# Phase features without GpSimd, tails added ahead of the query split, and context tiles on lasting semaphores, in a four-layer transformer kernel

## Chip, cores and metric

The kernel runs on one NeuronCore of a Trainium2 chip. The metric is the device time of one execution in microseconds (us). An execution is one launch of the whole network, and a time given as a median is that of three executions.

## What is computed

The reference takes x (32 sequences of 32 tokens, 256 channels, so 1024 tokens) and a context (32 sequences of 257 rows of 192 channels) through four layers. Each layer adds a cross attention, a self attention and a feed-forward part to x, each behind a layer norm. Three places matter here.

```python
# L0_attn: scores with a phase part, per head of 16 channels
q_amp = softplus(q) / sqrt(mean(softplus(q)**2) + 1e-6)        # k_amp likewise
q_phi = pi * tanh(x @ Wqp)                                     # k_phi likewise
phase = (q_amp*cos(q_phi)) @ (k_amp*cos(k_phi)).T + (q_amp*sin(q_phi)) @ (k_amp*sin(k_phi)).T
scores = (q @ k.T + 0.5*tanh(lambda_raw) * phase) / 4

# L2_xattn: softmax attention over the 257 context rows, 8 heads of 64 channels
out = softmax((x @ Wq) @ (context @ Wk).T / 8) @ (context @ Wv) @ Wo + bo

# L3_xattn: the same kind with one head of 256 channels
out = softmax((x @ Wq + bq) @ (context @ Wk + bk).T / 16) @ (context @ Wv + bv)
```

## The kernel before

The program is a row of stages. A stage is a block in which each engine has its own list of instructions with semaphore waits written out by hand. All engines end a stage together and the next one then begins. Tokens lie 128 to a tile (NT = 8 tiles of BT = 4 sequences). The function prepare (from L388) does the layer norm, the turn to channel-major form and the projections ahead of most stages. Its sync engine (SP) runs load_early (L376): it issues the transfers listed in early, then fetches a later stage's weights (fetch_weights, L240), and at L385 waits until all the early transfers have landed. That wait is part of the stage, so no engine goes on before it is over.

**phase_features** (L1630, in L0_attn) works on tensors of 128 partitions by 2048 elements, one for queries (u = 0) and one for keys (u = 1). VectorE (DVE) takes |q| (L1646), ScalarE (ACT) takes tanh of the phases (L1686) and exp of minus |q| (L1689), and DVE makes 1 + exp and its rounding error (L1649, L1652). ACT takes Ln (L1693), DVE adds the parts to the amplitude (L1656, L1659) and squares it (L1661). TensorE (PE) sums the squares of each head in 32 small matmuls for each u (L1730), ACT takes the square root (L1703), DVE the reciprocal (L1666), ACT spreads it over the channels of the head (L1708), and PE turns it (L1738). DVE multiplies the amplitude by it (L1671) and then sine and cosine by the amplitude (L1677, L1679). GpSimd (POOL) sets two constants, folds the tanh for the cosine in two passes (L1716, L1718), and multiplies one sine tensor (L1721). Sines are taken by ACT at L1697 and L1700.

**absorbed_attention** (L1116, L2_xattn) runs over 32 sequences n, four to a group. Each engine runs body(it, first, last) for two groups. For sequence n, PE turns the probabilities (turn_probs, L1175), makes the scores of n + 1 (L1168), turns the weighted context of n - 1 (turn_weighted, L1197), and weights the context rows of n (L1187). In the first two sequences of a group (j = 0, 1) it makes half of the next group's absorbed queries (L1155), in j = 2 the head outputs (L1209), and in j = 3 the output product (L1217). ACT takes the turned probabilities (L1269), the turned weighted context of n - 1 (L1281), the exponentials of n + 1 (L1263), the weighted context of n (L1275), and in j = 0, 1 the new queries (L1287). DVE's order is at L1403 to L1422. It begins with add_tails(n - 1) (L1377), which adds the 257th context row to the weighted context. The maxima of n + 1 (L1362), the rounding of context n + 2 (L1354, L1357), the reciprocals (L1367, L1369) and, in j = 0, 1, split_queries (L1386) come behind it.

**wide_cross_attention** (L2494, L3_xattn) runs over the eight tiles i with three slots for context tiles. A tile is 514 + 261 + 768 KB. The first three and the tails (768 KB) are loaded by the prepare ahead of it (L2774 to L2781), the others by its own SP when the slot comes free (L2508 to L2513), behind u_done. PE makes the queries of tiles 0 and 1 (L2525, L2528) and the scores of tile 0 (L2539), and then for each tile what is at L2577 to L2585: turn_probs(i), scores(i + 1), weighted_context(i), outputs(i - 1) (L2570), queries(i + 2), turn_weighted(i).

Of the kernel before, what the change touches and what calls it, by code (L numbers as in the profile page):

```python
# [23 lines left out]
P = 128  # L24
B, S, D = 32, 32, 256
T = B * S
NT = T // P
# [360 lines left out]
def prepare(k, src, z, ht=None, padded=None, jobs=(), token_major=(), gain=None, shift=None, w_at=None,  # L388
            early=(), clear_early=None, fold=None):
# [27 lines left out]
    with stage(k, names) as (block, s), ExitStack() as ctx:  # L417
# [26 lines left out]
        @block.sync  # L444
        def _(sp):
            load_early(k, sp, s, early)
# [669 lines left out]
def absorbed_attention(k, w, qt, given, rows):  # L1116
# [9 lines left out]
    with stage(k, names) as (block, s), \  # L1126
# [223 lines left out]
        def _(dve):  # L1350
# [84 lines left out]
            add_tails(B - 1, 1, NT - 1, BT - 1)  # L1435
# [194 lines left out]
def phase_features(k, w, qk, ph, amp, sn, cs):  # L1630
# [5 lines left out]
             "norm_done tanh_done rise_done fold_done sin_done cos_done lam_tanh lam_done const_done")  # L1636
    with stage(k, names) as (block, s), \
# [6 lines left out]
        def _(dve):  # L1644
            for u in range(2):
                nc.vector.scalar_tensor_tensor(amp[:, u], qk[:, u], -1.0, qk[:, u], ALU.mult, ALU.max).then_inc(s.abs_done, 1)  # L1646
            for u in range(2):
# [6 lines left out]
            for u in range(2):  # L1654
# [5 lines left out]
                dve.wait_ge(s.amp_done, u + 1)  # L1660
                nc.vector.tensor_tensor(b.f[:, u], amp[:, u], amp[:, u], ALU.mult).then_inc(s.square_done, 1)  # L1661
# [10 lines left out]
            dve.wait_ge(s.norm_done, 8)  # L1672
            dve.wait_ge(s.lam_done, 1)
            for done, t in ((s.sin_done, sn), (s.cos_done, cs)):
                dve.wait_ge(done, 2)
                for c in range(DC):
                    nc.vector.scalar_tensor_tensor(t[:, 0, c], t[:, 0, c], b.lam[:, 1, c:c + 1], amp[:, 0, c],  # L1677
                                                   ALU.mult, ALU.mult)
            nc.vector.tensor_tensor(cs[:, 1], cs[:, 1], amp[:, 1], ALU.mult)  # L1679

        @block.scalar
        def _(act):
            act.wait_ge(*w.at)
            nc.scalar.activation(b.lam[:, 0], w.lam, ACT.Tanh).then_inc(s.lam_tanh, 1)
            for u in range(2):
                nc.scalar.activation(ph[:, u], ph[:, u], ACT.Tanh).then_inc(s.tanh_done, 1)  # L1686
            for u in range(2):
                act.wait_ge(s.abs_done, u + 1)
                nc.scalar.activation(amp[:, u], amp[:, u], ACT.Exp, scale=-1.0).then_inc(s.exp_done, 1)  # L1689
            for u in range(2):  # L1690
# [3 lines left out]
            act.wait_ge(s.tanh_done, 2)  # L1694
# [14 lines left out]

        @block.gpsimd  # L1710
        def _(pool):
            nc.gpsimd.memset(b.eps[:], 1e-6).then_inc(s.const_done, 1)
            nc.gpsimd.memset(b.half[:], PI / 2).then_inc(s.const_done, 1)
            for u in range(2):
                pool.wait_ge(s.tanh_done, u + 1)
                nc.gpsimd.tensor_scalar(cs[:, u], ph[:, u], 0.0, 2.0, ALU.max, ALU.mult).then_inc(s.rise_done, 1)  # L1716
                pool.wait_ge(s.rise_done, u + 1)
                nc.gpsimd.tensor_tensor(cs[:, u], cs[:, u], ph[:, u], ALU.subtract).then_inc(s.fold_done, 1)  # L1718
            pool.wait_ge(s.norm_done, 8)
            pool.wait_ge(s.sin_done, 2)  # L1720
            nc.gpsimd.tensor_tensor(sn[:, 1], sn[:, 1], amp[:, 1], ALU.mult)  # L1721

        @block.tensor
        def _(pe):
            for u in range(2):
# [6 lines left out]
                mm.then_inc(s.sums_done, 1)  # L1732
            for u in range(2):
# [760 lines left out]
def wide_cross_attention(k, w, ht, given, turned, rows):  # L2494
# [6 lines left out]
    with stage(k, names) as (block, s), \  # L2501
# [20 lines left out]
        def _(pe):  # L2522
# [53 lines left out]
            for i in range(NT):  # L2576
# [78 lines left out]
def build(nc, args, packed, fields, order):  # L2655
# [7 lines left out]
    with ExitStack() as ctx:  # L2663
# [24 lines left out]
        k.weights_loaded = [ctx.enter_context(nc.semaphore(f"weights_loaded{h}")) for h in range(2)]  # L2688
        k.stored = ctx.enter_context(nc.semaphore("stored"))
# [152 lines left out]
```

## Time and profile before

| | us |
|---|---|
| median of three runs | 2164.79 |
| lowest and highest | 2161.39, 2168.08 |
| the profiled execution's own time | 2166.26 |
| its span in the trace | 2164.5 |
| PE busy | 1633.4 |
| DVE busy | 1021.2 |
| ACT busy | 732.4 |
| POOL busy | 479.7 |

The profile is of one execution. Times of rows are from the start of its span. Busy time of an engine is summed over its instructions. Where an engine's idle time ended by a signal, the profile names the engine and line that sent it, as [idle before <-releaser]. The granted clock (PEclk) is that of TensorE, 1.00 at 2.4 GHz and 0.50 at 1.2 GHz.

### The profile page before, as it was taken

The numbers are of one execution on the slowest core, as the hardware profiler recorded it, in microseconds if no ns is written. First come the engines' busy times: TensorE is split into PE (matmuls) and PEld (weight loads), VectorE is DVE, ScalarE is ACT, GpSimd is POOL, SyncE is SP. The second block draws the span as 40 slices with busy tenths as digits, with TensorE's granted clock in tenths as the row PEclk, the third lists the DMA queues.
The fourth block names the chain that finished last, engine by engine and source line by source line (L and its number), as shares of the span: only waits on it lengthen the run. The fifth ranks groups of instructions, "written<-read, shape, count | busy, mean of one in ns | idle before, by whom it ended". The sixth has DMA issues, their size and how long they took to land. (4 is left out here: it accounts for less than half of the span.)

```text
span 2164.5 us, 54009 instructions
## 1 busy us (share of the span) xinstructions
PE 1633.4 (75%) x21983; PEld 1404.8 (65%) x21983; DVE 1021.2 (47%) x2154; ACT 732.4 (34%) x1682; POOL 479.7 (22%) x634
## 2 busy tenths in 40 slices
PE   5998635769986999764888478867388968877684
PEld 4887534659974777654777367864277946655573
DVE  5655484241117888336111446554855734344314
ACT  3554331123333555221323245542223322332121
POOL 3442242002213343100444121200001200010241
PEclk9999755569997999765999789997697979676797
DMA  4110000049972111003999612210100153000584
GB/s 141 53 51 23 4 0 3 4 172 343 346 266 85 51 47 28 5 3 114 304 298 306 239 52 83 78 49 0 42 24 30 39 184 114 4 2 13 176 283 166
DMA packets 89649, 228.61 MB, mean 106 GB/s; under 512 B 20008, under 2 KB 42792, under 8 KB 81904
## 3 DMA queue, kind: packets, MB, share of 16 engines
q1 hardware_dynamic: 81296, 203.49, 28.5%
q0 software_dynamic: 8160, 22.29, 3.1%
q8 instruction: 152, 2.49, 0.5%
q14 instruction: 41, 0.34, 0.0%
HBM read 210.34 MB, written 15.34 MB: 104 GB/s over the span
## 5 line engine op out<-in xcount | busy, mean ns | idle before, releaser
L2215 PEld LDWEIGHTS ps<-xt,w 128*128 128x128 f32 x1728 | 212.6, 197 | 10.2 <-issue 4.0
L2215 PE MATMUL ps<-xt,w 128*128 128x128 f32 x1728 | 214.3, 281 | 2.5 <-DVE xt L2396 2.1
L2253 ACT ACTIVATE g<-ps,b 128x128 f32<-128x128 f32 x340 | 122.5, 367 | 272.7 <-PE ps L2215 253.0
L2225 PE MATMUL ps<-w,g 128*128 128x256 f32 x864 | 206.9, 388 | 0.0
L2225 PEld LDWEIGHTS ps<-w,g 128*128 128x128 f32 x864 | 160.7, 194 | 19.2
L2273 POOL DMA_INDIRECT x<-rows,token x85 | 83.3, 980 | 293.0 <-DVEq L2372 264.2
L2278 POOL DMA_INDIRECT results<-y,dest x85 | 83.7, 985 | 283.7 <-DVE y L2409 223.8
L2396 DVE COPY xt<-ps 128x256 f32<-128x256 f32 x85 | 36.1, 425 | 229.8 <-PE ps L2205 181.6
L472 PE MATMUL ps<-x,w 128*128 128x512 f32 x408 | 112.0, 433 | 19.5 <-DVE x L610 19.5
L454 PE MATMUL ps<-consts_sb,z_sb 128*128 128x128 f32 x176 | 41.3, 406 | 110.1 <-DVE z_sb L598 110.0
L454 PEld LDWEIGHTS ps<-consts_sb,z_sb 128*128 128x128 f32 x176 | 32.9, 210 | 119.9 <-DVE z_sb L598 116.6
L472 PEld LDWEIGHTS ps<-x,w 128*128 128x128 f32 x408 | 83.9, 211 | 40.9 <-DVE x L610 23.6
L785 PE MATMUL ps<-c,w 128*128 128x258 f32 x512 | 95.6, 299 | 8.5 <-DVE pt L1083 6.4
L795 PE MATMUL ps<-w,c 128*128 128x256 f32 x512 | 90.8, 290 | 0.0
L785 PEld LDWEIGHTS ps<-c,w 128*128 128x128 f32 x512 | 76.4, 193 | 21.7 <-issue 17.7
L2409 DVE TENSOR_TENSOR y<-ps,b 128x256 f32<-128x256 f32 x62 | 26.3, 425 | 131.8 <-PE ps L2225 131.8
L921 ACT ACTIVATE p<-sc,nmax 128x257 f32<-128x257 f32 x128 | 58.0, 503 | 78.5 <-DVE nmax L1048 78.5
L1036 DVE TENSOR_TENSOR val<-ps,store_sb 128x512 f32<-128x512 f32 x64 | 44.2, 691 | 83.5 <-PE ps L795 83.2
L1934 PE MATMUL ps<-x,w 128*128 128x512 f32 x288 | 77.5, 408 | 7.7 <-DVE w L2073 7.7
L1947 PEld LDWEIGHTS ps<-w,g 128*128 128x128 f32 x576 | 75.9, 194 | 9.3 <-issue 5.4
L1947 PE MATMUL ps<-w,g 128*128 128x256 f32 x576 | 77.5, 286 | 4.9 <-DVE g L2047 4.9
L579 POOL TENSOR_TENSOR w<-store_sb,w 128x512 fp32r<-128x512 f32 (+1 forms) x20 | 26.9, 1361 | 239.8 <-ACT w L511 239.8
(403 smaller groups left out, 3673.7 us busy)
## 6 DMA issues: line engine op xcount, KB each, us to landing
w<-in_L_ffn_w SPq DMA_DIRECT2D x124, 512.0 KB
w<-in_L_ffn_w SPq DMA_DIRECT2D x46, 1024.0 KB
c<-in_ctx SPq DMA_DIRECT2D x96, 258.0 KB, 2.8
b<-in_w_L_ffn SPq DMA_DIRECT2D x62, 128.0 KB
rows<-in_w_L_xattn SPq DMA_DIRECT2D x32, 192.0 KB
rows<-in_w_L_xattn SPq DMA_DIRECT2D x8, 768.0 KB
c<-in_w_L_xattn SPq DMA_DIRECT2D x8, 514.0 KB
back<-results SPq DMA_DIRECT2D x16, 256.0 KB, 5.2
```

What stands on the lines that cost most here:

```text
L454: mm = nc.tensor.transpose(k.ps[:, 2 * half + c, t * P:(t + 1) * P], z[:, half * HT + t, c * P:(c + 1) * P], k.ident)
L472: mm = nc.tensor.matmul(bank, r.w[:, p1, c, col:col + P], r.x[:, p2, c, half * 512:(half + 1) * 512], start=i == 0 and c == 0, stop=i == 2 ...
L785: last = nc.tensor.matmul(k.ps[:, KB + c, 0:LP], wp, cp, start=t == 0, stop=t == 4)
L795: last = nc.tensor.matmul(k.ps[:, VB, half * D:(half + 1) * D], cp, wp, start=t == 0, stop=t == 4)
L921: last = nc.scalar.activation(b.p[:, par, r4, :], score, ACT.Exp, bias=b.nmax[:, par, r4:r4 + 1])
L1934: mm = nc.tensor.matmul(k.ps[:, slot(j, h), :], r.w1[:, j // 2, p1, c, h * P:(h + 1) * P], r.x[:, p2, c, (j % 2) * 512:(j % 2 + 1) * 512], ...
L1947: mm = nc.tensor.matmul(k.ps[:, 4 + t, 0:D], r.g[:, p1, slot(j, h), t * P:(t + 1) * P], r.w2[:, j // 2, p2, h, :], start=h == 0 and i == 0 ...
L2215: mm = nc.tensor.matmul(hidden_bank(par, h), b.w1[:, par, c, h * P:(h + 1) * P], b.xt[:, par, c, :], start=c == 0, stop=c == DC - 1)
L2225: mm = nc.tensor.matmul(k.ps[:, YB + par, 0:D], b.g[:, par, h, :], b.w2[:, par, h, :], start=h == 0, stop=h == HC - 1)
L2253: nc.scalar.activation(b.g[:, par, h, :], hidden_bank(par, h), func, bias=b.b1[:, par, h:h + 1]).then_inc(s.g_ready, 1)
L2273: nc.gpsimd.indirect_dma_start(b.x[:, n % 2, :], None, k.rows, bass.IndirectOffsetOnAxis(ap=u.token[:, n:n + 1], axis=0)).then_inc(x_loade ...
L2278: nc.gpsimd.indirect_dma_start(k.results, bass.IndirectOffsetOnAxis(ap=u.dest[:, n:n + 1], axis=0), b.y[:, n % 2, :], None).then_inc(sent[ ...
```

## The change

**In phase_features** the POOL block is gone. DVE sets the two constants at its start. The two POOL passes of the fold become one Abs on ACT. The squares move from DVE to ACT (Square). The multiplication of sine and cosine by the amplitude and lambda moves ahead of the roots, and DVE then multiplies sine and cosine (16 pieces of 512) by the turned roots, where it multiplied the amplitude (8 pieces) before. PE waits for both roots ahead of the turn.

**In absorbed_attention** DVE adds the tails of n in the iteration of n, behind the reciprocals of n + 1 and ahead of split_queries.

**In L3_xattn** the context tiles of slot 0, the tails, and slots 1 and 2 are issued in this order on three semaphores that last over stages. The prepare no longer waits for them. PE waits for each slot ahead of its first use. queries(i + 2) goes ahead of outputs(i - 1).

```diff
-def load_early(k, sp, s, early):
+def load_early(k, sp, s, early, ahead=()):
+    for dst, src, done in ahead:
+        sp.dma_start(dst, src).then_inc(done, 16)
     for dst, src in early:
...
@@ absorbed_attention, DVE body
-                        if not (begin and j == 0):
-                            add_tails(n - 1, (j + 1) % 2, group if j else group - 1, (j - 1) % BT)
                         if not final:
                             maxima(n + 1, (j + 1) % 2)
                         if not (end and j >= 2):
                             round_context(n + 2, j % 2, 4 * it + 2 * gpar + j // 2 + 1)
                         if not final:
                             reciprocals(n + 1, (j + 1) % 2)
+                        add_tails(n, j % 2, group, j)
                         if j < 2 and not end:
                             split_queries(group + 1, 1 - gpar, j)
...
@@ phase_features, DVE (behind |q| of both u; plus(u) is L1649 and L1652, amplitude(u) L1656 and L1659)
+            for u in range(2):
+                plus(u)
             dve.wait_ge(s.lam_tanh, 1)
             nc.vector.tensor_scalar(b.lam[:, 1], b.lam[:, 0], 0.5, None, ALU.mult).then_inc(s.lam_done, 1)
             for u in range(2):
+                amplitude(u)
+            dve.wait_ge(s.amp_done, 2)
+            dve.wait_ge(s.lam_done, 1)
+            for done, t in ((s.sin_done, sn), (s.cos_done, cs)):
+                dve.wait_ge(done, 1)
+                for c in range(DC):
+                    nc.vector.scalar_tensor_tensor(t[:, 0, c], t[:, 0, c], b.lam[:, 1, c:c + 1], amp[:, 0, c],
+                                                   ALU.mult, ALU.mult).then_inc(s.scaled, 1)
+                dve.wait_ge(done, 2)
+                nc.vector.tensor_tensor(t[:, 1], t[:, 1], amp[:, 1], ALU.mult).then_inc(s.scaled, 1)
+            for u in range(2):
                 dve.wait_ge(s.root_done, u + 1)
                 nc.vector.reciprocal(b.rms[:, 1, u], b.rms[:, 0, u]).then_inc(s.recip_done, 1)
+            dve.wait_ge(s.scaled, 6)
             for u in range(2):
                 for q in range(4):
                     dve.wait_ge(s.wide_done, 4 * u + q + 1)
-                    part = amp[:, u, q // 2, (q % 2) * 512:(q % 2) * 512 + 512]
-                    nc.vector.tensor_tensor(part, part, k.ps[:, 4 * u + q, :], ALU.mult).then_inc(s.norm_done, 1)
+                    for t in (sn, cs):
+                        part = t[:, u, q // 2, (q % 2) * 512:(q % 2) * 512 + 512]
+                        nc.vector.tensor_tensor(part, part, k.ps[:, 4 * u + q, :], ALU.mult)
...
@@ phase_features, ACT, in its new order: lam, tanh 0, exp 0 and 1, then
+            nc.scalar.activation(ph[:, 1], ph[:, 1], ACT.Tanh).then_inc(s.tanh_done, 1)
+            for u in range(2):
+                act.wait_ge(s.tanh_done, u + 1)
+                nc.scalar.activation(cs[:, u], ph[:, u], ACT.Abs).then_inc(s.fold_done, 1)
...
             for u in range(2):
                 nc.scalar.activation(sn[:, u], ph[:, u], ACT.Sin, scale=PI).then_inc(s.sin_done, 1)
+            act.wait_ge(s.amp_done, 1)
+            nc.scalar.activation(b.f[:, 0], amp[:, 0], ACT.Square).then_inc(s.square_done, 1)
...
                 nc.scalar.activation(cs[:, u], cs[:, u], ACT.Sin, bias=b.half[:, 0:1], scale=-PI).then_inc(s.cos_done, 1)
+            act.wait_ge(s.amp_done, 2)
+            nc.scalar.activation(b.f[:, 1], amp[:, 1], ACT.Square).then_inc(s.square_done, 1)
...
@@ wide_cross_attention, PE
                 if i >= SLOTS:
                     pe.wait_ge(loaded[slot], 48 * (i // SLOTS))
+                else:
+                    pe.wait_ge(k.context_ahead[i], 64 if i == 0 else 48)
...
                 weighted_context(i)
+                if i + 2 < NT:
+                    queries(i + 2)
                 if i > 0:
                     outputs(i - 1)
-                if i + 2 < NT:
-                    queries(i + 2)
```

## Rows read from the trace of the kernel before

**Rows 1.** Stretches: start:end, length, busy us of each engine, granted clock, DMA share, GB/s.

```profile
262.20:336.90 74.70, 19.18 (x96) 18.85 (x96) 63.17 (x28) 28.15 (x19) 32.50 (x7) 0.56 0.00 0
302.00:318.00 16.00, 13.85 (x64) 13.75 (x64) 9.37 (x7) 7.67 (x7) 0.00 (x0) 0.50 0.00 0
480.00:640.00 160.00, 159.94 (x1102) 150.45 (x1101) 18.26 (x43) 62.30 (x176) 41.16 (x42) 1.00 0.93 333
1280.00:1440.00 160.00, 140.60 (x1208) 127.67 (x1207) 93.15 (x238) 90.58 (x256) 30.53 (x34) 1.00 0.29 80
1749.70:1761.70 12.00, 0.00 (x0) 0.00 (x0) 0.01 (x1) 0.00 (x0) 0.00 (x0) 0.50 0.95 333
```

The engines stand in the order PE, PEld (weight loads), DVE, ACT, POOL.

**Rows 2.** Timeline of the phase features: start, us, engine, line, operation, [idle before <-releaser].

```profile
262.22 4.49 DVE L1646 SCALAR_TENSOR_TENSOR amp<-qk 128x2048 f32<-128x2048 f32 x2 [0.33 <-PEq L219]
...
288.26 5.34 POOL L1718 TENSOR_TENSOR cs<-cs,ph 128x2048 f32<-128x2048 f32 x1
289.29 6.46 DVE L1652 SCALAR_TENSOR_TENSOR amp<-f,amp 128x2048 f32<-128x2048 f32 x1
...
295.85 1.91 ACT L1693 ACTIVATE f<-f 128x2048 f32<-128x2048 f32 x1 [11.32 <-DVE amp L1652]
297.78 1.28 ACT L1697 ACT_TABLE_LOAD   x1
...
316.54 0.37 ACT L1703 ACTIVATE rms<-ps,eps 128x128 f32<-128x128 f32 x1 [6.49 <-PE ps L1730]
...
319.90 0.69 DVE L1671 TENSOR_TENSOR amp<-amp,ps 128x512 f32<-128x512 f32 x1 [2.01 <-PE ps L1738]
```

**Rows 3.** Who waited for whom, 1258 to 1440: total us, times, longest us.

```profile
PE ps L1197 <- DVE u L1377: 20.0, 15, 1.4
...
PE ps L1175 <- ACT p L1263: 3.0, 5, 1.8
```

**Rows 4.** Timeline of the absorbed attention, one iteration with j = 1.

```profile
1337.15 0.66 PE L1175 MATMUL ps<-consts_sb,p 128*128 128x128 f32 x4
1337.27 1.08 ACT L1287 CAST q<-ps 128x512 fp32r<-128x512 f32 x2 [0.27 <-PE ps L1155]
...
1338.38 1.29 DVE L1386 TENSOR_TENSOR q<-ps,q 128x512 fp32r<-128x512 f32 x2 [1.61 <-ACT q L1287]
...
1339.58 0.74 DVE L1377 SCALAR_TENSOR_TENSOR u<-tails,u 128x192 f32<-128x192 f32 x2
1340.24 0.69 DVE L1362 TENSOR_REDUCE nmax<-ps 128x2 f32<-128x514 f32 x1
1340.38 0.65 PE L1197 MATMUL ps<-consts_sb,u 128*128 128x128 f32 x4 [1.36 <-DVE u L1377]
...
1341.55 0.48 ACT L1263 ACTIVATE p<-ps,nmax 128x257 f32<-128x257 f32 x1
...
1342.46 0.74 ACT L1275 ACTIVATE u<-ps,rsum 128x192 f32<-128x192 f32 x2
...
1343.36 0.66 PE L1175 MATMUL ps<-consts_sb,p 128*128 128x128 f32 x4
```

**Rows 5.** Timeline of L3_xattn: weights issued in the prepare, first matmul, scores, first refill.

```profile
1746.03 0.43 SPq L247 DMA_DIRECT2D store_sb<-in_w_L_attn  x1
...
1761.73 1.20 PE L2525 MATMUL ps<-ht_sb,qk 128*128 128x128 f32 x4 [12.75 <-PEq L219]
...
1765.42 1.31 PE L2539 MATMUL ps<-c,q 128*32 128x257 f32 x16
...
1772.87 0.33 SPq L2511 DMA_DIRECT2D c<-in_w_L_xattn  x1
...
1781.10 1.08 PE L2539 MATMUL ps<-c,q 128*32 128x257 f32 x16 [0.25 <-ACT q L2593]
...
1802.50 1.08 PE L2539 MATMUL ps<-c,q 128*32 128x257 f32 x16 [1.13 <-DMA rows<-in_w_L_xattn]
```

**Rows 6.** DMA issues from 1740 to 1765: size each, median us to landing.

```profile
store_sb<-in_w_L_attn SPq DMA_DIRECT2D x1, 1024.0 KB, 17.7
```

More of the change, by code:

```diff
@@ L388, in prepare @@
 def prepare(k, src, z, ht=None, padded=None, jobs=(), token_major=(), gain=None, shift=None, w_at=None,
-            early=(), clear_early=None, fold=None):
+            early=(), clear_early=None, fold=None, ahead=()):
     nc = k.nc
@@ L445, in _ @@
         def _(sp):
-            load_early(k, sp, s, early)
+            load_early(k, sp, s, early, ahead)
         @block.tensor
@@ L1434, in _ @@
             body(NT // 2 - 1, False, True)
-            add_tails(B - 1, 1, NT - 1, BT - 1)
             take_outputs(NT - 1)
@@ L1635, in phase_features @@
     names = ("abs_done exp_done plus_done rest_done ln_done sum_done amp_done square_done sums_done root_done recip_done spread_done wide_done "
[L1636 removed]
+             "tanh_done fold_done sin_done cos_done lam_tanh lam_done const_done scaled")
     with stage(k, names) as (block, s), \
@@ L1644, in _, with plus @@
         def _(dve):
-            for u in range(2):
-                nc.vector.scalar_tensor_tensor(amp[:, u], qk[:, u], -1.0, qk[:, u], ALU.mult, ALU.max).then_inc(s.abs_done, 1)
-            for u in range(2):
+            def plus(u):
                 dve.wait_ge(s.exp_done, u + 1)
@@ L1653, in _, with amplitude @@
                                                ALU.subtract).then_inc(s.rest_done, 1)
-            for u in range(2):
+            def amplitude(u):
                 dve.wait_ge(s.ln_done, u + 1)
@@ L1659, in _ @@
                 nc.vector.tensor_tensor(amp[:, u], b.f[:, u], amp[:, u], ALU.subtract).then_inc(s.amp_done, 1)
-                dve.wait_ge(s.amp_done, u + 1)
-                nc.vector.tensor_tensor(b.f[:, u], amp[:, u], amp[:, u], ALU.mult).then_inc(s.square_done, 1)
+            nc.vector.memset(b.eps[:], 1e-6).then_inc(s.const_done, 1)
+            nc.vector.memset(b.half[:], PI / 2).then_inc(s.const_done, 1)
+            for u in range(2):
+                nc.vector.scalar_tensor_tensor(amp[:, u], qk[:, u], -1.0, qk[:, u], ALU.mult, ALU.max).then_inc(s.abs_done, 1)
+            for u in range(2):
+                plus(u)
             dve.wait_ge(s.lam_tanh, 1)
@@ L1669, in _ @@
                     dve.wait_ge(s.wide_done, 4 * u + q + 1)
-                    part = amp[:, u, q // 2, (q % 2) * 512:(q % 2) * 512 + 512]
-                    nc.vector.tensor_tensor(part, part, k.ps[:, 4 * u + q, :], ALU.mult).then_inc(s.norm_done, 1)
[L1672 to L1679, printed above, removed]
+                    for t in (sn, cs):
+                        part = t[:, u, q // 2, (q % 2) * 512:(q % 2) * 512 + 512]
+                        nc.vector.tensor_tensor(part, part, k.ps[:, 4 * u + q, :], ALU.mult)
         @block.scalar
@@ L1684, in _ @@
             nc.scalar.activation(b.lam[:, 0], w.lam, ACT.Tanh).then_inc(s.lam_tanh, 1)
-            for u in range(2):
-                nc.scalar.activation(ph[:, u], ph[:, u], ACT.Tanh).then_inc(s.tanh_done, 1)
+            nc.scalar.activation(ph[:, 0], ph[:, 0], ACT.Tanh).then_inc(s.tanh_done, 1)
             for u in range(2):
@@ L1689, in _ @@
                 nc.scalar.activation(amp[:, u], amp[:, u], ACT.Exp, scale=-1.0).then_inc(s.exp_done, 1)
+            nc.scalar.activation(ph[:, 1], ph[:, 1], ACT.Tanh).then_inc(s.tanh_done, 1)
+            for u in range(2):
+                act.wait_ge(s.tanh_done, u + 1)
+                nc.scalar.activation(cs[:, u], ph[:, u], ACT.Abs).then_inc(s.fold_done, 1)
             for u in range(2):
@@ L1708, in _ @@
                 nc.scalar.copy(roots(u).rearrange("p a (h d) -> p (a h) d", d=16), spread(inverse, 16, 2)).then_inc(s.spread_done, 1)
[L1710 to L1721, printed above, removed]
         @block.tensor
@@ L1732, in _ @@
                 mm.then_inc(s.sums_done, 1)
+            pe.wait_ge(s.root_done, 2)
             for u in range(2):
@@ L2688, in build @@
         k.weights_loaded = [ctx.enter_context(nc.semaphore(f"weights_loaded{h}")) for h in range(2)]
+        k.context_ahead = [ctx.enter_context(nc.semaphore(f"context_ahead{n}")) for n in range(3)]
         k.stored = ctx.enter_context(nc.semaphore("stored"))
@@ L2777, in build @@
                     for n in range(3):
-                        given += [(b.c0[:, n], turned[:, n, 0]), (b.c1[:, n], turned[0:DK + 1 - P, n, 1]),
-                                  (b.rows[:, n], rows[:, n])]
+                        given += [(b.c0[:, n], turned[:, n, 0], k.context_ahead[n]),
+                                  (b.c1[:, n], turned[0:DK + 1 - P, n, 1], k.context_ahead[n]),
+                                  (b.rows[:, n], rows[:, n], k.context_ahead[n])]
+                    given.insert(3, (b.tails[:].rearrange("p i d -> p (i d)"), tails, k.context_ahead[0]))
                     prepare(k, k.x, k.z, ht=k.ht, w_at=w.at, fold=(w.wq, w.wk, w.bq, b.qk[:], b.bqk, 1.0 / 16),
-                            early=given + [(b.tails[:].rearrange("p i d -> p (i d)"), tails)])
+                            ahead=given)
                     wide_cross_attention(k, w, k.ht, b, turned, rows)
```

1 line of the change is left out of this document (removed).

## Prediction

> **What bounds the kernel now.** I read the page first. PE is busy for 75% of the span, but that is a mean over a chain of stages, and what an edit is worth must be read in its own stage. So I took the busy time of each stretch next [rows 1], and there the three places differ.
>
> In the phase features (262.2 to 336.9, 74.7 us) DVE is busy 63.2 us and PE 19.2. The work is a dependent chain between DVE, ACT and PE. The timeline [rows 2] shows why DVE is so busy. The two-input pass L1646 takes 2.25 us for 2048 elements, but L1652, also two-input and of the same shape, takes 6.46 while POOL runs L1718 beside it. Thus ACT waits 11.32 us for DVE before the second Ln. In the absorbed attention PE is busy 140.6 of 160 us at clock 1.00 [rows 1]. I read the waits there [rows 3]. The one PE wait of size is that of L1197 for the tails of DVE, 20.0 us in 15 times. In L3_xattn I read the timeline [rows 5]. The first matmul of the attention starts at 1761.7, PE having been idle for 12.75 us. From 1749.7 to there no engine computes, and DMA is 95% busy [rows 1]. This is the wait of L385 for the context tiles.
>
> **Part A, phase features.** POOL's work leaves, so I cost DVE at the uncontended row, 2.3 for a two-input pass of 2048 (L1646), and ACT at 1.9 for a pass (L1693) [rows 2]. Placed from 262.2 on:
> - ACT: a table load (1.28) and lambda to 263.6, tanh to 265.5, two exponentials to 269.3, tanh to 271.2, two Abs to 275.0. DVE's two constants (0.1 us) are hidden, since ACT comes to its first exp at 265.5 and |q| is there at 264.6.
> - DVE: 1 + exp and its error for both u, from 267.4. The one-input pass has no clean row. It is bounded by 1.1 (half of a two-input one) and 2.3. With 2.3 the first pair is ready at 272.0 and the second at 276.6. ACT comes to its Ln at 276.3, behind a table load, and to the second at 278.2. So this unknown costs nothing at either end.
> - ACT: two Ln to 280.1, table load and two sines to 285.2, Square 0 to 287.1 (its amplitude is ready at 278.2 + 4.6 = 282.8), two cosines to 290.9, Square 1 to 292.8.
> - PE: the 64 matmuls of the sums took 13.85 us at clock 0.50, with PE busy throughout [rows 1]. I keep that: 287.1 to 294.0, and to 300.9. DVE meanwhile finishes the amplitudes (287.4) and the products of sine and cosine with them (four passes' worth, 9.6 with the split in two, to 297). These stood behind the roots before and now hide behind PE.
> - The end: the sums end at 300.9 where they ended at 316.5. The first product with the turned roots started 3.4 us behind them (319.9 against 316.5) [rows 2], so it starts at 304.3. It is 16 pieces at 0.69, or 11.0, where it was 8. The stage ends near 315.6 instead of 336.9.
>
> A gives 21.3 us. The new wait of PE for both roots holds nothing back, since the spread on ACT stands behind both roots as it is.
>
> Square is on no row, nor is Abs. Their pass I take at 1.9. Open is whether they need a table of their own. From below that costs nothing; from above it is three more loads of 1.28, so 3.9 us. I take nothing, as the nearest case is tanh and exp, which share one load at the start of this stage. The trace has the sine start at 299.06, right behind the load, and the load right behind the end of Ln (297.76), so a switch costs 1.3 [rows 2]. The Trainium skill (ScalarE: Activation LUTs, What ACT_TABLE_LOAD costs) gives about 2.66 us for every switch, with a drain; by that three more would cost 8.0 us. No drain shows in the row, so I go by the row. The skill (same page, Table sets) says that cheap functions such as abs are in every set, and doesn't list Square there.
>
> **Part B, absorbed attention.** No instruction is added; only DVE's order changes. With j = 1 (and j = 2) PE's turn of the weighted context comes late because add_tails stands behind split_queries, which waits for ACT's new queries. In the rows the split starts at 1338.38, the tails at 1339.58, and PE turns at 1340.38, 1.36 late [rows 4]. After the change the tails of n need the weighted context alone, which ACT ends 0.16 before PE's next turn of probabilities (1342.46 + 0.74 against 1343.36), so in this iteration at 1337.0. They end at 1337.8, before the new queries come to DVE at 1338.38. The split isn't delayed, and PE's wait goes.
>
> What is late next? Walk round the loop of ACT and DVE: exponentials 0.91 (1341.55 to 1342.46), weighted context 0.74, new queries 1.08, split 1.29, maxima 0.69, signals about 0.15: 4.86 us [rows 4]. PE's iteration was 6.21 (1337.15 to 1343.36) and becomes 4.85 without the wait. They are equal, so a small wait may be left, which I put at 0.1 in each. With j = 2 and j = 3 PE has long products besides, and the loop has no queries in it. DVE's new wait for the weighted context has split and the output copies queued behind it, and both are due later anyway. Context transfers have slack, with DMA 29% busy [rows 1].
>
> B gives 20.0 less 1.0, so 19.0 us. The bounds are 10 (the loop takes half back) and 21.
>
> **Part C, L3_xattn.** The prepare's work ends at 1749.7 and the attention starts at 1750.0, not 1761.7. The first scores come 3.7 us behind [rows 5], at 1753.7. Is the data there? The transfers run from about 1742 at 333 GB/s [rows 1]. Slot 0 and the tails are 2.37 MB, 7.1 us, so they land near 1749.3. Slot 1 lands near 1754 and slot 2 near 1759, each some 3 us before its scores. The weights issued behind them at 1746.03 landed 17.7 us later, at 1763.7 [rows 5, 6]. That they landed behind the tiles speaks for service in order. The refill of slot 0 is issued at 1772.9 now and at about 1761.2 then. It queues some 2 us behind those weights, about the start-up that it has anyway. From there to the last scores DMA sets the pace, since PE waits 1.13 us for it at the last tile [rows 5], and that stretch keeps its length. The swap of outputs and queries removes PE's wait of 0.25 us for queries [rows 5], six times at most; as DMA ends the stretch, I count it as nothing.
>
> C gives 11.7 less 0.4 for the queueing, so 11.3 us. The bounds are 3.7 (all slots land together at 1761 and only the queries overlap) and 13.5 (the clock rises sooner, PE being idle for less).
>
> **Sum.** 21.3 + 19.0 + 11.3 = 51.6 us. Against the profiled execution's 2166.3 (its span is 2164.5) that is 2114.7. This execution lies 1.5 above the median, so I forecast 2113.
>
> **Rivals.**
> - *The loop of ACT and DVE becomes the bound of B.* For it: 4.86 against 4.85. Against it: PE shows only 3.0 us of waits for the exponentials [rows 3]. B gives 10, the time is 2122. Chance 0.12.
> - *Table loads eat into A.* Three more of 1.28, and up to 2 us of waiting behind them, make 6. For it: Square isn't shown. The time is 2119. Chance 0.10.
> - *The slots don't land in order*, so C gives 3.7. Against it: where the weights landed. The time is 2121. Chance 0.08.
> - *The clock.* From 480 to 640 (L0_ffn) PE is busy throughout at clock 1.00 [rows 1], so a stretch at 0.50 there costs half of its length. The earlier parts reach that stage sooner and with other idle times, and the clock might rise later. The kernel becomes slower than before if PE-bound stretches of over 104 us that are now at 1.00 run at 0.50, which gives back the 52; for all 160 us it is +80, and 2193. Against it: PE is busier after the change in all three places. Chance 0.02.
> - *More than forecast.* The sums of squares at clock 1.00 would take half, and other stretches now at 0.50 may rise sooner: 10 us more, 2103. Chance 0.05.
>
> The forecast has the rest, 0.63, and its own range is 2107 to 2119 (2 us of spread between runs, 3 for clock shifts, 1 for B). Reaching out to the three rivals of less gain, I give 2105 to 2123. A measurement here tells 0.3%, some 6.5 us, from no change. All cases but the clock lie well below that, so faster has 0.97, the same 0.01, slower 0.02.
>
> **What would show it.** In the profile after: L1652 at 2.3 us; the phase stage 53 us long, with PE's sums from near 287 and no load ahead of Square. In the absorbed attention, the wait of L1197 for L1377 under 3 us, and the stage 19 shorter. In L3_xattn, the first L2525 within 1 us of the prepare's last copy, no wait over 1 us ahead of the first three scores, and the last scores still waiting for DMA. Wrong would be a new wait of L1175 for L1263 of 10 us in total, a wait ahead of scores 0, or L0_ffn at a clock under 1.00.

## The result, and the profile after

| | before | after |
|---|---|---|
| median, us | 2163.22 of 4 runs (2161.39 to 2168.08) | 2105.76 of 4 runs (2103.08 to 2109.45) |
| profiled execution (its span) | 2166.26 (2164.5) | 2106.90 (2105.1) |

The ratio is 0.9722, with a 95% interval of 0.969 to 0.9755. On the 2164.79 shown before the prediction that is 2104.6 us. The forecast was 2113, the range began at 2105. So the change is faster by 2.8% where 2.4% was predicted: the sign and the three places were right, and the gain was put too small by 8 us.

The page of the kernel after begins so:

```profile
span 2105.1 us, 54013 instructions
## 1 busy us (share of the span) xinstructions
PE 1622.7 (77%) x21983; PEld 1397.9 (66%) x21983; DVE 999.9 (47%) x2163; ACT 742.9 (35%) x1686; POOL 447.3 (21%) x627
```

To see where the time went, I took the length of each stage from the two traces, from its first DVE instruction to that of the next stage (A from the pass that takes |q|, as the two constants now stand 0.03 us ahead of it). The edited stages, in us:

| stage | before | after | gain | predicted |
|---|---|---|---|---|
| A, phase features | 75.27 | 51.40 | 23.9 | 21.3 |
| B, absorbed attention | 200.55 | 176.66 | 23.9 | 19.0 |
| C, L3_xattn with its prepare | 71.88 | 60.52 | 11.4 | 11.3 |

Together they give 59.1 of the 59.4 us between the two spans. The other stages nearly cancel out, but not all of them keep their length: the self attention of L3_attn alone went from 54.95 to 58.89 us with no edit (more of this below).

**A.** The timeline of the phase features after (start, us, engine, line, operation, [idle before <-releaser]):

```profile
267.03 1.23 DVE L1647 TENSOR_SCALAR f<-amp 128x2048 f32<-128x2048 f32 x1 [0.53 <-ACT amp L1696]
268.29 2.29 DVE L1649 SCALAR_TENSOR_TENSOR amp<-f,amp 128x2048 f32<-128x2048 f32 x1
...
270.50 3.69 ACT L1700 ACTIVATE cs<-ph 128x2048 f32<-128x2048 f32 x2
...
279.24 1.28 ACT L1707 ACT_TABLE_LOAD   x1
...
280.53 3.71 ACT L1707 ACTIVATE sn<-ph 128x2048 f32<-128x2048 f32 x2
...
284.15 1.89 ACT L1709 ACTIVATE f<-amp 128x2048 f32<-128x2048 f32 x1
...
286.09 13.82 PE L1731 MATMUL ps<-consts_sb,f 128*128 128x8 f32 x64 [25.20 <-ACT f L1709]
...
299.95 0.37 ACT L1717 ACTIVATE rms<-ps,eps 128x128 f32<-128x128 f32 x1 [6.46 <-PE ps L1731]
...
303.44 0.69 DVE L1687 TENSOR_TENSOR sn<-sn,ps 128x512 f32<-128x512 f32 x1 [2.14 <-PE ps L1740]
304.05 0.68 DVE L1687 TENSOR_TENSOR cs<-cs,ps 128x512 f32<-128x512 f32 x1
304.65 0.68 DVE L1687 TENSOR_TENSOR sn<-sn,ps 128x512 f32<-128x512 f32 x1
...
312.42 0.68 DVE L1687 TENSOR_TENSOR cs<-cs,ps 128x512 f32<-128x512 f32 x1
```

The two-input pass (L1649 now) takes 2.29 us where it took 6.46 beside POOL [rows 2]. The one-input pass, which had no clean row, takes 1.23. In the kernel before, it was stretched further still, as its timeline shows:

```profile
265.56 8.10 POOL L1716 TENSOR_SCALAR cs<-ph 128x2048 f32<-128x2048 f32 x1 [2.98 <-ACT ph L1686]
...
269.10 5.64 DVE L1649 TENSOR_SCALAR f<-amp 128x2048 f32<-128x2048 f32 x1 [2.39 <-ACT amp L1689]
273.75 5.34 POOL L1718 TENSOR_TENSOR cs<-cs,ph 128x2048 f32<-128x2048 f32 x1
274.78 6.46 DVE L1652 SCALAR_TENSOR_TENSOR amp<-f,amp 128x2048 f32<-128x2048 f32 x1
279.06 9.11 POOL L1716 TENSOR_SCALAR cs<-ph 128x2048 f32<-128x2048 f32 x1
281.16 8.09 DVE L1649 TENSOR_SCALAR f<-amp 128x2048 f32<-128x2048 f32 x1
```

In these rows each DVE pass ends behind the POOL pass that ran beside it, and by about its own clean time: L1649 1.08 us behind the end of L1716 both times (274.74 and 273.66, 289.25 and 288.17; 1.23 clean), L1652 2.15 us behind the end of L1718 both times (281.24 and 279.09, 295.75 and 293.60; 2.29 clean). So the rows read as if DVE waited for the POOL pass to end and then took its own clean time: what it paid here was the rest of the POOL pass.

In the kernel after, the Abs (L1700) and the Square (L1709) follow the work before them with no load in between. The sums begin 24.1 us behind the start of the stage (286.09 - 262.00), where the forecast had 24.9 (287.1 - 262.2). The 16 products start 0.60 us apart, though each is 0.68 long: the next one starts 0.08 before the last has ended.

**B.** The timeline of one iteration with j = 1 in the kernel after, with the same columns:

```profile
1302.91 0.66 PE L1177 MATMUL ps<-consts_sb,p 128*128 128x128 f32 x4
1302.97 0.75 DVE L1379 SCALAR_TENSOR_TENSOR u<-tails,u 128x192 f32<-128x192 f32 x2 [0.44 <-ACT u L1277]
...
1304.13 1.29 DVE L1388 TENSOR_TENSOR q<-ps,q 128x512 fp32r<-128x512 f32 x2 [0.42 <-ACT q L1289]
...
1304.25 0.53 PE L1170 MATMUL ps<-c,q 128*128 128x258 f32 x3
...
1304.61 0.60 PE L1199 MATMUL ps<-consts_sb,u 128*128 128x128 f32 x4
...
1307.54 0.66 PE L1177 MATMUL ps<-consts_sb,p 128*128 128x128 f32 x4
```

The tails (L1379) now end before the split (L1388) begins, and the turn (L1199) carries no idle time where it carried 1.36 [rows 4]. It even starts 0.17 before the modelled end of the scores (1304.25 + 0.53 = 1304.78). So the iteration went from 6.21 us to 4.63 (1302.91 to 1307.54), by 1.58 and not by 1.36; the 1.36 of idle time and the 0.17 of overlap are 1.53 of it. PE's waits in this stage after, from 1234 to 1404 (total us, times, longest), answer to [rows 3]:

```profile
PE ps L1177 <- ACT p L1265: 3.4, 5, 1.8
PE ps L1170 <- DVE q L1388: 2.5, 1, 2.5
```

No row is left for L1199. From 1258 to 1452, up to the end of its stage, the kernel before had

```profile
PE ps L1197 <- DVE u L1377: 21.2, 16, 1.4
```

The window of [rows 3] ended at 1440 and missed the sixteenth wait. Fourteen of the sixteen stand in the iterations with j = 1 and 2 and add up to 19.2 us; the two others, 0.86 and 1.17 us, stand at the end of the stage.

**C.** The timeline of L3_xattn after, the same columns, answering to [rows 5]:

```profile
1697.31 0.69 DVE L619 COPY ht_sb<-ps 128x512 f32<-128x512 f32 x1 [0.50 <-PE ps L456]
1698.30 1.20 PE L2527 MATMUL ps<-ht_sb,qk 128*128 128x128 f32 x4 [1.03 <-PEq L219]
...
1701.98 1.94 PE L2543 MATMUL ps<-c,q 128*32 128x257 f32 x16
1705.89 1.08 PE L2543 MATMUL ps<-c,q 128*32 128x257 f32 x16
...
1709.07 0.33 SPq L2513 DMA_DIRECT2D c<-in_w_L_xattn  x1
...
1711.72 1.08 PE L2543 MATMUL ps<-c,q 128*32 128x257 f32 x16 [0.25 <-ACT q L2597]
...
1717.78 1.08 PE L2543 MATMUL ps<-c,q 128*32 128x257 f32 x16 [1.18 <-DMA rows<-in_w_L_xattn]
...
1734.57 1.07 PE L2543 MATMUL ps<-c,q 128*32 128x257 f32 x16 [1.60 <-DMA rows<-in_w_L_xattn]
```

The first matmul comes 0.3 us behind the prepare's last copy (1698.00), the first scores 3.7 behind it, and none of the first three scores waits for DMA. Those of tiles 3, 5 and 6 do, 3.3 us in all; those of tile 7 (1739.42) follow without a wait. The stretches of the kernel after (columns of [rows 1]) complete this:

```profile
286.09:299.91 13.82, 13.82 (x64) 13.73 (x64) 10.65 (x8) 7.19 (x5) 0.00 (x0) 0.50 0.00 0
454.30:614.30 160.00, 160.00 (x1103) 150.87 (x1102) 18.24 (x43) 64.63 (x176) 41.16 (x42) 1.00 0.93 332
1698.00:1709.00 11.00, 9.21 (x70) 5.66 (x70) 2.00 (x7) 3.65 (x9) 0.33 (x3) 0.66 1.00 327
1709.00:1736.00 27.00, 23.40 (x238) 16.24 (x235) 8.92 (x27) 7.45 (x23) 0.00 (x0) 0.97 0.95 288
```

The sums stayed at 0.50. L0_ffn, at the same distance from its start as in [rows 1], stayed at 1.00.

### The profile page after: what moved, and what is told of

The parts are those of the page before. It is cut to its first block and busy times, and to the rows that moved or that the text cites. A ratio compares the mean times of both kernels' runs of the same rounds, so it can differ in the third digit from the quotient of the medians.

```text
span 2105.1 us, 54013 instructions
## 1 busy us (share of the span) xinstructions
PE 1622.7 (77%) x21983; PEld 1397.9 (66%) x21983; DVE 999.9 (47%) x2163; ACT 742.9 (35%) x1686; POOL 447.3 (21%) x627
## 5 line engine op out<-in xcount | busy, mean ns | idle before, releaser
L474 PEld LDWEIGHTS ps<-x,w 128*128 128x128 f32 x408 | 83.3, 210 | 41.0 <-DVE x L612 23.9
```

The lines of the kernel that those rows point to most:

```text
L474: mm = nc.tensor.matmul(bank, r.w[:, p1, c, col:col + P], r.x[:, p2, c, half * 512:(half + 1) * 512], start=i == 0 and c == 0, stop=i == 2 ...
```

## The experiments

My theory was that the three parts add up, each by its own mechanism: A by DVE passes without POOL beside them and by work moved behind PE's sums, B by the wait of L1197 alone, C by the early start. The rivals: clock shifts in other stages hold part of the 59 us; B's gain is bounded by the loop of ACT and DVE; C's by the weights ahead of the refills. Runs with only one part come first.

**One part at a time.** *a1* makes the edits of phase_features alone; it is the kernel after with B and C taken back:

```diff
 # a1_features, against the kernel after
+                        if not (begin and j == 0):
+                            add_tails(n - 1, (j + 1) % 2, group if j else group - 1, (j - 1) % BT)
...
-                        add_tails(n, j % 2, group, j)
...
-                    pe.wait_ge(k.context_ahead[i], 64 if i == 0 else 48)
```

> The kernel before with the new phase features alone. Theory (the three parts are independent and add up): the phase stage goes from 75.0 us (start to start of the next stage) to 51.5 as in the profile after, and the whole loses 23 to 26 us. The margin is the L0 self attention behind it, which was 96.9 long before and 95.0 after: if that difference comes from this edit it is 95.0 here too, if it is chance of the clock it can be anything from 94 to 98. Rival (the parts are not independent, the profile after owes something to their sum): the whole moves by another amount than the stage.

It took 2141.40 us (median of 5), the ratio 0.9897 [0.9863, 0.9932]. The phase stage is 51.40 long, exactly as after. The self attention behind it took 98.3 us, where before had 96.6 and after 95.0, with no edit to it; so that difference does not come from A.

*b1* moves the tails alone:

```diff
 # b1_tails, against the kernel before
-                        if not (begin and j == 0):
-                            add_tails(n - 1, (j + 1) % 2, group if j else group - 1, (j - 1) % BT)
...
+                        add_tails(n, j % 2, group, j)
                         if j < 2 and not end:
```

> The kernel before with the tails of n added in iteration n, and nothing else. Theory: the whole absorbed stage loses 23.9 us as in the profile after; iterations with j = 1 and j = 2 lose 1.58 us each, where the wait of the turn for the tails is shown with 1.36. Rival: some of the 23.9 comes from an earlier or later stage, and the stage alone loses 19 to 20, as the sum of the waits says.

It took 2134.77 us (median of 4), the ratio 0.9874 [0.9838, 0.991]. The absorbed stage is 177.84 long, against 200.55. That is 1.2 us less of a gain than the 23.9 expected. The iterations with j = 1 and 2 have the lengths of the kernel after (4.63 and 5.43 us). What is missing lies in the very first iteration, which took 6.85 us at a mean granted clock of 0.58, against 5.71 at 0.70 after; in *d1* (below), which does not touch this stage, it took 6.78.

*b3* adds the tails early only where a split follows, so that only the iterations change whose turn waited:

```diff
 # b3_two, against the kernel before
-                        if not (begin and j == 0):
+                        if not (begin and j == 0) and (j == 0 or j == 3 or end):
...
                         if j < 2 and not end:
+                            add_tails(n, j % 2, group, j)
                             split_queries(group + 1, 1 - gpar, j)
```

> The kernel before with the tails moved only in the iterations that have a split of queries (j = 0 and j = 1 of all groups but the last); in the others they stay at the start of the next iteration. Theory one (each of the 15 waits costs more than its row shows, since PE also loses the overlap of one group of matmuls with the next): j = 1 and j = 2 lose 1.58 each and the stage loses 22 us or a little more. Theory two (the waits are worth the 20.0 us of their row, and the rest is gained in the iterations with j = 3 and j = 0, and at the stage's end): this kernel loses 20 or less, and the one with all tails moved loses 4 more.

It took 2141.53 us (median of 7), the ratio 0.992 [0.9891, 0.9949]. From the first start of turn_probs to the thirty-second it is 151.76 us, as after (151.55) and b1 (152.73), against 173.66 before. The stage lost 20.6 us, which is between the two theories, because the part behind the thirty-second start is 14.54 long, against 13.27 before and 11.49 after. PE's waits from 1248 to 1432 show one cause:

```profile
PE ps L1197 <- DVE u L1377: 2.0, 2, 1.2
```

These are the two waits at the end of the kernel before, 0.86 and 1.17 us, and what they cost is the 1.8 us between 13.27 and 11.49. The other 1.3 us in b3 are no wait: its last head outputs took 3.24 us (1.97 before) for the same 32 matmuls, at a mean granted clock of 0.58 (1.00 before).

```profile
1422.22 3.24 PE L1209 MATMUL ps<-ut,store_sb 128*64 128x128 f32 x32 [0.68 <-ACT ut L1281]
```

Thus nearly all of B, 21.8 us between before and after, sits in the iterations with j = 1 and 2, and 1.8 us are the same wait at the end of the stage.

*c1* loads the tiles ahead and keeps the old order of outputs and queries; *d1* makes that swap alone:

```diff
 # c1_ahead, against the kernel before (load_early issues ahead first, as in the change)
+                else:
+                    pe.wait_ge(k.context_ahead[i], 64 if i == 0 else 48)
...
+                            ahead=given)
 # d1_swap, against the kernel before
-                if i > 0:
-                    outputs(i - 1)
                 if i + 2 < NT:
                     queries(i + 2)
+                if i > 0:
+                    outputs(i - 1)
```

> The kernel before with the context tiles of the last cross attention on lasting semaphores, queries and outputs in their old order. Theory (DMA ends this stage): the stage with its prepare is 60.5 us long against 71.9 before, as in the profile after with the swapped order; the last scores wait for the rows, and the steps between scores are 5.1 us where no transfer is waited for. Rival (the swap gives part of the 11.4): the stage is 61.5 to 62 long here.

> The kernel before with queries(i + 2) ahead of outputs(i - 1) in the last cross attention, and nothing else. Theory (transfers end that stage, so the swap alone is worth nothing): the steps between scores go from 5.13 to 4.86 us where no transfer is waited for, the waits for transfers grow by the same, and the stage with its prepare stays within 0.5 us of 71.9. Rival: it loses 5 x 0.27, so 70.5.

c1 took 2153.9 us (median of 10), the ratio 0.9959 [0.9928, 0.9989], and its L3_xattn is 60.73 long. d1 took 2166.01 in one execution, where 11 of the kernel before on the same chip have a median of 2168.33, and its stage is 71.76 long, before 71.88. In runs whose L3_xattn is that of the kernel before, the stage took 71.1 to 71.9 us. The rival for d1, 70.5, lies outside of this, so the early start is the whole of C as far as can be seen, and the swap is worth nothing that shows. The three ratios multiply to 0.9897 x 0.9874 x 0.9959 = 0.973, against 0.9722 measured for the whole. Each of them is known to 6 to 8 us on either side only, so it is the lengths of the stages that show that the parts add up, and the product merely agrees.

**Inside A.** *a2* is the kernel before with only the fold taken from POOL:

```diff
 # a2_fold, against the kernel before; ACT:
+            for u in range(2):
+                act.wait_ge(s.tanh_done, u + 1)
+                nc.scalar.activation(cs[:, u], ph[:, u], ACT.Abs).then_inc(s.fold_done, 1)
 # POOL:
-            for u in range(2):
-                pool.wait_ge(s.tanh_done, u + 1)
-                nc.gpsimd.tensor_scalar(cs[:, u], ph[:, u], 0.0, 2.0, ALU.max, ALU.mult).then_inc(s.rise_done, 1)
-                pool.wait_ge(s.rise_done, u + 1)
-                nc.gpsimd.tensor_tensor(cs[:, u], cs[:, u], ph[:, u], ALU.subtract).then_inc(s.fold_done, 1)
```

> The kernel before, with only the cosine's fold moved from GpSimd's two passes to an Abs on ScalarE behind the exponentials. GpSimd keeps the two constants and the last sine product. Theory (most of the 23.9 us of the phase stage is VectorE being held up beside GpSimd): L1652 takes 2.3 us instead of 6.46 and the one-input pass 1.2; the sums of squares start near 283 instead of 302.7, and what follows them keeps its 20.4 us, so the stage is about 56 long, 19.5 less than before. The rest of the 23.9, some 4.4, is then the move of the products behind the sums. Rival (half or more comes from the squares on ScalarE and the moved products): the stage stays over 63.

One execution took 2141.02 us, one of the kernel before beside it 2164.91, and the stage is 57.78 us long: the fold's two POOL passes for each u were alone worth 17.5 of A's 23.9. I had expected some 56, from sums that start 20.8 us behind the start of the stage (283 - 262.2); they start 22.5 behind it (283.25 - 260.74). One POOL pass is left in it, and DVE pays for that one too, as its timeline shows:

```profile
283.25 13.85 PE L1728 MATMUL ps<-consts_sb,f 128*128 128x8 f32 x64 [23.57 <-DVE f L1661]
...
306.52 6.82 DVE L1677 SCALAR_TENSOR_TENSOR sn<-sn,lam,amp 128x1024 f32<-128x1024 f32 x2
306.56 4.49 POOL L1719 TENSOR_TENSOR sn<-sn,amp 128x2048 f32<-128x2048 f32 x1 [45.46 <-DVE amp L1671]
```

L1677 takes 6.82 us beside POOL, where the same two halves take 2.47 in the cosine's line. The new order and the last POOL pass hold the other 6.4. No run takes these two apart; the 4.35 us between 6.82 and 2.47 stand on the chain to the end of the stage, so I estimate that most of the 6.4 is the last POOL pass.

*a4* goes beyond the change: ACT spreads the root of u = 0 and PE turns it before the sums of u = 1 have their root.

```diff
 # a4_spread, against the kernel after
-            pe.wait_ge(s.root_done, 2)
             for u in range(2):
+                if u == 1:
+                    pe.wait_ge(s.root_done, 2)
                 pe.wait_ge(s.spread_done, u + 1)
 # and on ACT the spread of u = 0 stands ahead of the root of u = 1
```

> The kernel after, with ScalarE spreading the first root ahead of the second root, and TensorE turning it without waiting for the second. Theory (the end of the phase stage is VectorE's 16 products, which start when the first spread is turned): they start near 301 instead of 303.4, half of them are done when the second spread comes, and the stage is 49.0 long instead of 51.4. Rival (the second spread, its turn and its 8 products end last, whatever the first does): from the second root at 300.0 there are 0.95 of reciprocal, 1.9 of spread, 1.2 to the first turned piece and 8 products of 0.6, to 309, so the stage would be 47.5 to 49 too, and only a start of the second half's products right behind the first's tells them apart.

The first product starts earlier (timeline of a4), and the stage is 49.11 long; one execution took 2097.41 us:

```profile
299.27 4.07 PE L1746 MATMUL ps<-consts_sb,f 128*128 128x128 f32 x17
...
300.73 0.63 DVE L1687 TENSOR_TENSOR sn<-sn,ps 128x512 f32<-128x512 f32 x1
...
304.85 0.68 DVE L1687 TENSOR_TENSOR cs<-cs,ps 128x512 f32<-128x512 f32 x1
305.45 0.68 DVE L1687 TENSOR_TENSOR sn<-sn,ps 128x512 f32<-128x512 f32 x1
```

The last two rows are the eighth and the ninth product. The ninth, the first of u = 1, starts right behind, which is the sign by which the expectation told its theory from the rival. So what ends the stage after is the chain from the sums to 16 products on DVE, as the prediction placed it.

**Inside B.** *b2* puts two needless DVE passes behind the split, to see whether the loop of ACT and DVE (4.86 us by my sum) sets the length of an iteration:

```diff
 # b2_pass, against the kernel after
                             split_queries(group + 1, 1 - gpar, j)
+                            for g in range(NG):
+                                tail = given.tails[:, j, ds(group, 1), :].rearrange("p a d -> p (a d)")
+                                nc.vector.tensor_tensor(b.idle[:, g, :], tail, tail, ALU.add)
```

> The kernel after, with two more passes of VectorE of 128x192 (some 0.74 us in all, their result is not used) behind every split of queries. It asks how near the loop of ScalarE and VectorE, put at 4.86 us in the prediction, is to TensorE's 4.63. Theory one (the loop has slack, because only two iterations in a row have queries in it and TensorE's long products follow): iterations with j = 1 grow by 0.3 to 0.4, those with j = 2 by nothing, the stage by 2 to 3 us. Theory two (the loop is the bound already): j = 1 and j = 2 grow by 0.74 each, the stage by 10.

One execution took 2117.99 us. Its timeline shows what the passes add:

```profile
1312.22 0.62 DVE L1419 TENSOR_TENSOR idle<-tails 128x192 f32 x2
1312.76 0.68 DVE L1364 TENSOR_REDUCE nmax<-ps 128x2 f32<-128x514 f32 x1
```

They take 0.62 us, and from their start to that of the next pass it is 0.54, less than the 0.74 that I had expected. From one start of turn_probs to the next, the iteration with j = 1 went from 4.63 to 4.76 us and that with j = 2 from 5.43 to 5.49, so 0.13 and 0.06 of the 0.54 were passed on. A loop that bound the iteration would have passed on all of it. From the first start of turn_probs to the last it is 2.6 us more (154.19 against 151.55); 1.1 of these lie in the first iteration (6.80 us), which took 6.85 in b1 and 6.78 in d1 without any such pass. PE's waits for the exponentials rose only from 3.4 to 4.2 us in all:

```profile
PE ps L1177 <- ACT p L1265: 4.2, 5, 1.8
```

The rest of this run's 12 us over after lies elsewhere: the unedited self attention of L0 alone was 5.4 us longer.

**Inside C.** *c2* leaves the context rows out of the refills of tiles 3 to 7, and so half of their bytes; tiles 3 to 7 then use the old rows. *c3* issues the next stage's weights behind the refills and not ahead of them:

```diff
 # c2_light, against the kernel after
-                sp.dma_start(given.rows[:, slot], rows[:, i + SLOTS]).then_inc(loaded[slot], 16)
 # c3_weights_last, against the kernel after, load_early
-    fetch_weights(k, sp)
+    if not ahead:
+        fetch_weights(k, sp)
 # and behind the refills of wide_cross_attention
+            fetch_weights(k, sp)
```

> The kernel after without the transfers of the context rows (768 KB a tile) in the five refills, so tiles 3 to 7 are weighted with the rows of tiles 0 to 2. Theory (transfers set the pace of the last cross attention from tile 3 on): the waits of the scores for transfers, 3.3 us, go, all steps between scores are 4.86 us, and the stage is 57 long instead of 60.5. Rival (TensorE sets the pace and the transfer waits are covered by other work): 60.5 stays.

> The kernel after, with the 1 MB of the next stage's weights issued behind the five refills instead of between the first three tiles and the refills. Theory (transfers set the pace of the whole stage, so 1 MB less ahead of the last tile is 1.05 MB at 310 to 330 GB/s): the waits of 3.3 us go and the stage is 57.2 to 57.5 long; the weights land near 1742, before the next stage wants them at 1749, so nothing is paid back. Rival (the weights are late for the next stage): its prepare grows by as much.

c2 (one execution, 2112.30 us) has no wait for DMA in the stage, its later scores start 4.81 us apart, and the stage is 55.30 long, expected 57. Of the difference 1.6 lies between the scores of tiles 1 and 2, which start 4.26 us apart (5.83 after), as in c1 and b2, which refill everything; so it is no effect of the edit, and what makes it 4.26 or 5.83 stays open. The 3.3 us of waits that are gone show that the data of the refills is the bound of the last part. c3 took 2112.32 us (median of 4), the ratio 0.9747 [0.9718, 0.9775], and its stage is 60.12 long. Here my expectation of some 57 failed. The timeline and the stretch of c3 up to its first refill show why:

```profile
1711.28 0.33 SPq L2514 DMA_DIRECT2D c<-in_w_L_xattn  x1
```

```profile
1699.00:1711.00 12.00, 9.48 (x72) 5.63 (x70) 2.69 (x8) 4.25 (x10) 0.33 (x3) 0.64 0.77 263
```

The first refill is issued 20.3 us behind the stage's first transfer in c3 (1711.28 - 1690.96) and in after (1709.07 - 1688.80), because it waits for tile 0 to be used. In the 11 or 12 us up to there DMA is busy 1.00 of the time in after and 0.77 in c3. So the weights had filled transfer time that nothing else could use, and moving them made the DMA idle instead.

*e1* joins a4 and c3:

> The kernel after with both: the first root spread ahead of the second (if that gave 2.4 us) and the weights behind the refills (3.2 us). Theory: the two stages are 49.0 and 57.3 long, and the whole is some 5.5 us faster than the kernel after, so 0.9695 of the kernel before; single executions spread by more than that, so the stage lengths decide and not the medians.

2105.33 us (median of 6, 2099.74 to 2112.49), the ratio 0.9721 [0.9694, 0.9747]. Its stages are 49.13 and 60.68 us long, near those of the two apart (49.11 and 60.12); the 57.3 expected of the second failed with c3. The 2.3 us of a4 (51.40 - 49.11) are too little to be told from no change, and no kernel here is measurably better than the change itself.

## Why the prediction was right in kind and wrong in size

- **A, predicted 21.3, measured 23.9.** The mechanism held. L1652 took 2.29 (2.3 forecast), the one-input pass 1.23 (bounds 1.1 to 2.3, and no cost either way), the sums 13.82 at 0.50, the first product came 3.5 us behind their end (3.4 forecast). The failed term is "16 pieces at 0.69, or 11.0": they start 0.60 apart, and the last one ends 9.66 us after the first starts (303.44 to 313.10). That is 1.3 us. ACT's passes overlap by about 0.09 likewise (284.15, then 285.95, for a pass of 1.89), and the first product came 0.7 us sooner behind the start of the stage than forecast (41.4 us for 42.1). I had added up durations along the chain. The rest of the 2.6 us is in the sum itself: 304.3 + 11.0 is 315.3 and not 315.6, and it leaves out that the next stage begins 0.3 us behind the last pass of this one, where it began 0.6 behind in the kernel before.
- **B, predicted 19.0, measured 23.9.** The step that failed is "20.0 less 1.0", in both of its terms. First, the 20.0 was idle time between modelled ends, 19.2 of it in the 14 iterations with j = 1 and 2. Thirteen of these became 1.57 or 1.58 us shorter, and the one of the first group with j = 2, which has no head outputs, 1.26 (5.48 to 4.22): 21.8 in all, where their waits were 1.35 to 1.38 each. With the spread of the other iterations the loop gave 22.1. The two waits at the end of the stage, of which my window held 0.86, gave 1.8. Second, the 1.0 deducted for the loop of 4.86 us was never paid, since the iteration runs at 4.63. Only two iterations in a row carry queries, and b2 shows that at least 0.4 us of slack is left in each (0.54 added, 0.13 and 0.06 passed on). The upper bound of 21 was too low for the same reasons.
- **C, predicted 11.3, measured 11.4.** Start, first scores and the swap's worth of nothing came as forecast, and DMA still set the pace behind the refills: its waits at the scores came to 3.3 us in 3 times, though not at the last tile. The first refill came 12.1 us sooner behind the stage's first transfer (11.7 forecast), and from there to the last scores it took 0.7 us longer (0.4 forecast). That the two leave the total within 0.1 us is luck: the same code gave this stage 71.1 to 71.9 us in the old form, and 59.5 (a4), 60.5 and 61.4 (b2) in the new one.
- **The rivals.** The loop as the bound of B is refuted by b2 (0.13 and 0.06 us passed on of 0.54). More table loads did not come: the sines start at 280.53, 0.01 behind the end of their load, and Abs and Square need none. The drain that the Trainium skill (ScalarE: Activation LUTs, What ACT_TABLE_LOAD costs) counts in its 2.66 us for a switch shows in no row here; a switch cost 1.3 us. That all slots land together is refuted: the scores of tile 0 start without a wait 13.2 us behind the first transfer (1701.98 - 1688.80), and the 5.5 MB of the three slots and the tails take 16.6 us at 333 GB/s (an estimate by the rate in [rows 1]). When each slot landed is on no row. The weights behind them took 18.0 us from their issue, as they had (17.7) [rows 6]. L0_ffn kept its clock. The price that I had put on that rival was too low by half: by the ratio of the two levels, work that fills 160 us at 1.00 would take 320 at 0.50 (an estimate), so +160 and not +80, and 52 us of such work would have given the gain back, not 104. The rival "more than forecast", 2103, was nearest to the time, though not by its cause, for the sums stayed at 0.50.
- **The range.** It was drawn from the spread between runs, clock shifts, 1 us for B and the rivals that lessen the gain. The two mis-sized terms of A and B, 2.6 and 4.9 us, both lie on the side of more gain, where the range had 8 us of room; they put the time at 2104.6, below the 2105 at which it began. In one comparison the 17 executions of the kernel before lay between 2148.47 and 2175.88, and the measured ratio is known to 0.3%, some 7 us on either side, so the last 0.4 us mean nothing by themselves. The 7.5 us in A and B do: the stages kept these lengths in the other runs with the same code (51.4 in all of A, 176.7 to 178.1 for B).

## What to carry to other kernels

Price a chain by the distances between starts of a like chain in the trace, and take an idle time as the least that a removed wait can give, counting the waits up to the end of the stage: durations and idle times read the gain too small, here by a fifth in B (19.0 of 23.9). GpSimd passes beside a DVE chain must be priced on DVE too: here a DVE pass ended only behind the GpSimd pass beside it, which made 6.46 us of 2.29 and up to 8.09 of 1.23. Removing a barrier ahead of transfers is worth the time up to the point where the next resource, here a slot coming free and then its refill, sets the pace, and what is queued in idle transfer time costs nothing (c3).

## What was not expected of the hardware

Stages that no edit touches vary between executions with the granted clock, though nothing in them changed. The self attention of L0 over 95.00 us of the kernel after and over 100.40 us of b2, with the same 2768 matmuls:

```profile
313.40:408.40 95.00, 68.69 (x2768) 57.62 (x2768) 24.58 (x58) 20.45 (x42) 15.06 (x17) 0.60 0.02 4
```

```profile
312.90:413.30 100.40, 72.32 (x2768) 60.22 (x2768) 24.53 (x56) 20.39 (x42) 15.06 (x17) 0.55 0.02 4
```

DVE, ACT and POOL are busy for the same time in both; PE is not, at 0.60 and 0.55. L3_ffn lay between 171.9 and 182.5 us over these kernels in the same way. An effect of a few us must therefore be read from its own stage and not from one total. Secondly, PE was busy throughout the 64 small matmuls of the sums and yet had 0.50, half of 2.4 GHz, for 13.8 us in each of four traces (before, after, a2, a4). In all four it had been idle for over 23 us before them. What decides between the levels was not settled by these runs.
